# The first image's first eight score units taken from the unstacked parts, and its first value tiles moved behind four units

## What is computed

```python
xn = _group_norm(xf, gn_w, gn_b)
qkv = einsum('oc,bcl->bol', w_qkv, xn) + b_qkv[None, :, None]
q, k, v = ...                       # 8 heads of ch = 32 channels
weight = einsum('bct,bcs->bts', q * scale, k * scale)
weight = softmax(weight.astype(float32), axis=1)
a = einsum('bts,bcs->bct', weight, v)
h = einsum('oc,bcl->bol', w_proj, a) + b_proj[None, :, None]
x = xf + h
```

## Time and profile before

| | |
|---|---|
| median of 3 runs | 1343.61 us (1343.59 to 1346.18) |
| the profiled execution | 1351.87 us |
| its span, first to last instruction | 1350.1 us |
| TensorE busy | 1234.0 us (91%) |
| VectorE busy | 996.0 us (74%) |
| ScalarE busy | 878.0 us (65%) |
| mean granted TensorE clock | 0.984 of full |

### The profile page before, as it was taken

One profiled execution on the slowest core, in us unless ns is written; L12 is line 12 of the kernel. 1 busy time (PEld: TensorE's weight loads), 2 busy tenths in 40 slices (PEclk: granted clock), 3 DMA queues, 4 the chain that ended last, 5 costly groups with the idle time before them and its releaser, 6 DMA issues.

```text
span 1350.1 us, 22293 instructions
## 1 busy us (share of the span) xinstructions
PE 1234.0 (91%) x8028; PEld 646.0 (48%) x8028; DVE 996.0 (74%) x1609; ACT 878.0 (65%) x1457; POOL 466.6 (35%) x621
## 2 busy tenths in 40 slices
PE   6888899899998999899998999989998999979898
PEld 5544544544445454444444444454544444444465
DVE  3677688847888587866888578884879678794583
ACT  1567677676776668576775767766686767757332
POOL 2001017510384015630275203840156301751161
PEclk9999999999999999999999999999999999999999
DMA  8142325133442236223451234422362234410210
GB/s 275 47 123 67 98 59 114 25 68 117 100 108 59 46 99 141 49 63 94 98 114 25 66 118 100 108 50 49 106 141 49 63 94 99 81 27 0 80 33 32
DMA packets 51181, 110.86 MB, mean 82 GB/s; under 512 B 15456, under 2 KB 15840, under 8 KB 50816
## 3 DMA queue, kind: packets, MB, share of 16 engines
q1 hardware_dynamic: 48400, 100.39, 30.5%
q0 software_dynamic: 2480, 8.78, 2.3%
q10 hardware_dynamic: 192, 0.26, 0.1%
HBM read 21.81 MB, written 8.39 MB: 22 GB/s over the span
## 4 chain that ended last, share of the span: by engine, by line
PE 52%; DVE 29%; ACT 8%; issue 5%; POOL 3%; SPq 2%; DMA 1%; DVEq 0%; POOLq 0%; ACTq 0%
DVE negmax L1069 15%; PE ps_s L666 12%; PE ps_o L681 7%; PE work L754 6%; ACT probs L930 5%; PE work L693 5%; PE work L815 4%; PE work L740 4%; PE work L820 3%; PE work L705 3%; DVE tok L1145 3%; DVE ln_st L1134 3%; PE work L796 1%; DVE lo L1114 1%; PE work L728 1%
## 5 line engine op out<-in xcount | busy, mean ns | idle before, releaser
L1069 DVE TENSOR_REDUCE negmax<-ps_s 128x1 f32<-128x1024 f32 x512 | 619.4, 1214 | 219.2 <-PE ps_s L666 217.6
L930 ACT ACTIVATE probs<-ps_s,negmax 128x1024 f32<-128x1024 f32 x512 | 570.0, 1114 | 319.6 <-DVE negmax L1069 315.0
L666 PE MATMUL ps_s<-q_st,k_st 128*128 128x512 f32 x1024 | 407.3, 481 | 51.3 <-ACT probs L930 39.0
L666 PEld LDWEIGHTS ps_s<-q_st,k_st 128*128 128x128 f32 x1024 | 163.8, 191 | 294.0 <-ACT probs L930 161.2
L1347 POOL TENSOR_TENSOR v_scaled<-v_tok,rsums 128x128 f32<-128x128 f32 x128 | 55.9, 437 | 572.7 <-DVE rsums L1075 572.7
L681 PE MATMUL ps_o<-probs,v_scaled 128*32 128x512 f32 x2048 | 250.0, 606 | 1.3 <-POOL v_scaled L1347 1.3
L693 PE MATMUL work<-xg,w_qkv 128*128 128x512 f32 x256 | 121.0, 597 | 2.9 <-ACT xg L943 2.8
L754 PE MATMUL work<-ln_ch,w_qk 128*128 128x512 f32 x236 | 113.1, 601 | 3.4 <-DVE k_ch L1253 3.4
L681 PEld LDWEIGHTS ps_o<-probs,v_scaled 128*32 128x32 f32 x2048 | 53.8, 110 | 128.6 <-issue 116.6
L1406 POOL TENSOR_TENSOR x<-x,csum 128x1024 f32<-128x1024 f32 x45 | 107.5, 2389 | 2.5
L930 ACT ACTIVATION_READ_ACCUMULATOR probs<-ps_s,negmax 128x1 f32 x512 | 99.5, 194 | 0.0
(11 more groups left out here) (165 smaller groups left out, 1445.5 us busy)
## 6 DMA issues: line engine op xcount, KB each, us to landing
q_st<-hi SPq DMA_DIRECT2D x128, 128.0 KB, 2.4
q_st<-lo SPq DMA_DIRECT2D x120, 128.0 KB, 2.4
k_st<-t SPq DMA_DIRECT2D x224, 64.0 KB, 2.0
k_st<-hi SPq DMA_DIRECT2D x128, 64.0 KB, 2.0
k_st<-lo SPq DMA_DIRECT2D x128, 64.0 KB, 2.0
x<-in_x SPq DMA_DIRECT2D x8, 1024.0 KB, 6.0
out_x<-ln_ch SPq DMA_DIRECT2D x16, 512.0 KB, 2.8
xg<-in_x POOLq DMA_DIRECT2D x7, 1024.0 KB, 8.6
```

The lines of the kernel that those rows point to most:

```text
L666: mm = pe.matmul(ps_s[s % 2][:, half * HALF:half * HALF + HALF], k_st[:, h, j * P:j * P + P], q_st[g][:, h, half * HALF:half * HALF + HALF ...
L930: act.activation(probs[:, j % 2, h, :], ps_s[s % 2][:, :], ACT.Exp, bias=negmax[:, s % 4:s % 4 + 1], accum_out=sums[:, j % 2, h:h + 1]).th ...
L1069: dve.tensor_reduce(negmax[:, s % 4:s % 4 + 1], ps_s[s % 2][:, :], AX_X, ALU.max, negate=True)\
```

## The change

Four edits, all of the first image:

1. Units 0 to 7 (`DIRECT = 2 * HG`) are scored from `hi`, `lo`, `hi_first` and `lo_first` themselves: for each half of the queries four products of 32 rows by 512 columns accumulate in PSUM, so eight products stand for two. They wait for the parts in SBUF and not for the stacking DMAs. The stacked tensors are first read by unit 8. All DMAs stay.
2. The two tiles `pv0` leave the prologue of TensorE and VectorE. TensorE makes them in slots 3 and 4 of the first body, behind the scores of units 4 and 5; VectorE adds their bias behind the maxima of units 4 and 5.
3. `pv1` moves from TensorE's slot 0 (both parts) to slots 5 and 7, and on VectorE from slots 1 and 3 to 6 and 8. The warm entries of slots 0 to 4 go.
4. `hi_first` and `lo_first` lie in `q_st[1]` in place of `att`. So SyncE, before it stacks the second head group's queries of the first image, waits until the later half of the keys has been stacked.

```diff
-    "w1": (25, 27), "pq1": (11, 12), "pv1": (0, 0), "pk1": (19, 20), "gn": (39,), "pq0": (43, 44),
+    "w1": (25, 27), "pq1": (11, 12), "pv1": (5, 7), "pk1": (19, 20), "gn": (39,), "pq0": (43, 44),
...
-    "warm": (0, 1, 2, 3, 4, 5, 7, 8, 9, 13, 15, 16, 17, 21, 23, 24, 28, 29, 31, 32, 33, 35, 36, 37, 40, 41, 47, 48, 51, 52, 53, 57, 59, 60, 61),
+    "warm": (5, 7, 8, 9, 13, 15, 16, 17, 21, 23, 24, 28, 29, 31, 32, 33, 35, 36, 37, 40, 41, 47, 48, 51, 52, 53, 57, 59, 60, 61),
...
-    "invert": (4, 8, 12, 16, 20, 24, 28, 32, 36, 40, 44, 48, 52, 56, 60), "w1": (27, 29), "pv1": (1, 3),
+    "invert": (4, 8, 12, 16, 20, 24, 28, 32, 36, 40, 44, 48, 52, 56, 60), "w1": (27, 29), "pv1": (6, 8),
...
+DIRECT = 2 * HG
+VALUES_LATER = {HG - 1: ("pv0", 0), HG: ("pv0", 1)}
...
-        hi_first, lo_first = (att[:, n, :].bitcast(F32R) for n in range(2))
+        hi_first, lo_first = (q_st[1][:, n, :] for n in range(2))
...
         def stack_q(eng, b, g):
             eng.wait_ge(lo_done, 8 * b + 4 * g + 2)
+            if first_k(b, 0) and g == 1:
+                eng.wait_ge(k_stacked_b, 16 * DMA)
...
                 if first_k(i, g):
-                    if j == 0:
+                    if s < DIRECT:
+                        direct_scores(s, j, h)
+                        return
+                    if j == DIRECT // HG:
...
+            def direct_scores(s, j, h):
+                pe.wait_ge(lo_done, 1 + max(nth_split(0, t) for t in (("pk0", 0), ("pq0", 0), ("pq0", 1))))
+                if s >= 2:
+                    pe.wait_ge(probs_ready, s - 1)
+                rows, keys = slice(D * h, D * h + D), slice(P * j, P * j + P)
+                for half in range(2):
+                    cols = slice(half * HALF, half * HALF + HALF)
+                    for n, (k_part, q_part) in enumerate(((hi_first, hi), (lo_first, hi), (hi_first, lo), (lo_first, lo))):
+                        mm = pe.matmul(ps_s[s % 2][:, cols], k_part[rows, keys], q_part[rows, cols],
+                                       start=(n == 0), stop=(n == 3))
+                mm.then_inc(scores_ready, 1)
...
-                for tile in FIRST_TILES:
+                for tile in FIRST_TILES[:5]:
...
+                    if kind == "first" and s in VALUES_LATER:
+                        writing["body"] = -1
+                        pre_tile("prologue", -1, VALUES_LATER[s])
+                        writing["body"] = i
...
-                for tile in FIRST_TILES[1:]:
+                for tile in FIRST_TILES[1:5]:
...
+                    if kind == "first" and s - 1 in VALUES_LATER:
+                        writing["body"] = -1
+                        values(-1, VALUES_LATER[s - 1])
+                        writing["body"] = i
```

## The result

The changed kernel takes 1357.51 us (median of 6 runs, 1354.89 to 1362.92), the kernel before 1346.64 us beside it: ratio 1.0082, 95% interval 1.0063 to 1.0101. Its profiled execution took 1355.6 us with a span of 1353.8 us and a mean clock of 0.985.

A forecast was written before the change was run, and what follows sets the result against it. Query-stacking DMAs, then slow `pv1`, bound the first 50 us. The 6.85 us head start is spent by unit 9 (50.28 against 50.24); unit 11 gains 0.3 us: 1343.61 - 0.3 = 1343.3 us, range 1341.8 to 1347.8.

The forecast's parts named there:

- What bounded the stretch before: First 50 us: 7.94 us of DMA for stacked queries, then 5.22 us of `pv1` at the slow level, before unit 2.
- The price of a 32-row product: Direct units on TensorE: 0.23 us a product taken, between bounds of 0.213 and 0.31.
- Rivals 1: Direct units: slower by a dearer 32-row product; at 0.31 us each the time is 1346.5 us; chance 0.12.
- rival 3: Direct units: slower, weight loads not hidden within a row group, 40 x 0.11 = 4.4 us, 1347.7 us; chance 0.06.
- Rival 4: Direct units: faster, 32-row products run side by side and the 6.85 us head start is kept, 1336.8 us; chance 0.05.
- The changes of array form: Units 4 to 9 on TensorE: eight changes of form at about 0.1 us each, 0.8 us together.
- the gain of 0.3: Unit 11 at 53.56 us against 53.85 before, a gain that stays to the end of the kernel.
- The six warm pairs: Removed from slots in which TensorE waited: 2.6 us of TensorE work whose removal costs nothing.
- the slow stretch goes: 30 to 40 us: low clock should go, TensorE's pauses being only 25.4 to 26.9 and 30.5 to 31.6; sum at full clock.
- Rival 2: Direct stretch: slower by the clock; low throughout adds 8 us for products, 3.5 for value tiles (2.71 a pair), 1354.8; chance 0.05.
- SyncE's new wait and the stacking DMAs were covered: First image: wait ends about 44 us, parts behind it exist after 60; stacked queries issued at 31.19, needed at 47.5.
- nothing waits for a time of its own: Behind unit 11 the programs are the same, so the 0.3 us gain stays to the end.

The follow-up runs named there:

- e1: Changed kernel, but each product of a direct unit takes all 128 rows instead of its head's 32; 1.0018 of the kernel before.
- e3: Changed kernel with the direct scores alone, value tiles and warm entries back in their old places; 1.0096 of the kernel before.
- e6: The changed kernel, unchanged, run again for a second profile; 1.0069 of the kernel before.
- e9: Changed kernel with small 128-row filler products behind each of the first four direct units; 1.0079 of the kernel before.
- e7: Changed kernel with four direct units (0 to 3) in place of eight, all else the same; 0.9973 of the kernel before.
- e12: Changed kernel with four direct units and value tiles moved to TensorE's pauses, second run of that version; 0.9964 of the kernel before.

## Why the prediction was wrong

- What bounded the stretch before (DMAs, then `pv1` at the low clock), and that the waits go: right. Unit 0 began at 21.18 (forecast 21.57), unit 2 at 26.82 (26.95).
- The price of a 32-row product, 0.23 us: right at full clock, a unit being 1.84 us without its changes of form. Rivals 1 and 3, which stood on a dearer product, fall. All eight products of a unit are in one row group, and their loads are hidden at steps of 0.23. The trace so disagrees with the rule on weight loads that rival 3 came from (the Trainium skill, "TensorE: Matmul & The Clock Gate", Part 3, The mechanism). Rival 4 is half right: such products do run side by side, but those of two units and not of one, and off the path.
- The changes of array form: mis-sized. A direct unit is 2.03 and a value tile 1.98 in the chains, 4.01 a pair; in e1, where the form stays, a pair takes 3.63 (unit 5 at 34.70, unit 6 at 38.33). That is 0.19 for each change, not 0.1: 0.7 us over eight. With this alone the gain of 0.3 would have been a loss of 0.4, still no change. The six warm pairs that go are five, which cost nothing either way.
- **The step that failed** is the sentence that the slow stretch goes "since TensorE's pauses are now" short, with a sum made at full clock. It put the lower clock at nothing. Measured, it stretched a direct unit from 2.04 to 3.75 us and a value tile from 1.98 to 3.70, for 13.7 us in one profile and 30.7 in the other, and so put unit 11 5.1 and 13.3 us behind. I took pauses as the cause of a low clock. In e1 there are pauses and the clock is full; in e3 there is none and it falls and stays low. What differs in e1 is that the products use all 128 rows.
- Rival 2 had the mechanism's effect (low for the whole direct stretch, 1354.8 us) but not its cause, and so a chance of 0.05. It priced 11.5 us, and the medians say 10.9 and 6.3; the two profiles, at 5.1 and 13.3 us, lie around it. That is partly luck. Its value tile of 2.71 us is half of a term that ran only in part at the lower level; one wholly at that level takes 3.70. With five units at 1.71 and four tiles at 1.72 more, the whole stretch at the lower level would be 15.4 us, and no profile had all of it there.
- Behind unit 11 nothing gave the time back: right. SyncE's new wait and the stacking DMAs were covered: right, the distance to the kernel before is 5.1 us at unit 11 and still 5.1 at unit 63. That "nothing waits for a time of its own" behind it is too strong, as stays at the lower level come and go there.

The Trainium skill says on the clock ("TensorE: Matmul & The Clock Gate", Part 1, What's actually happening) that a monitor sets it by how busy the engine has been. Read as the busy share of the trace, that rule would give the direct units of e3 the full clock, and e3 disagrees: 5.00 of 5 us busy at 0.50.

What stays open: how often the low stretch is some 14 and how often some 30 us, as each kernel has one or two profiles; why the part behind unit 11 differs by up to 10.8 us between profiles, which is where the moved value tiles alone lost their 0.4%; what ends a low stretch, for the same units with value tiles between them ran at the lower level in e6 and at the full one in e9; and whether rows are the only thing that differs between the 32-row and the 128-row products, for e1 also stays in one array form and no products run side by side in it.

## What to carry to other kernels

Before a 128-row product is split into products of 32 rows to get round a wait, price the stretch at the lower clock too: a TensorE that is fully busy with narrow products can run at half speed for as long as they last, and drags the full-width work between them along. Use such products as a bridge only (here four units, not eight), and look at the granted clock of the stretch beside the busy share. Full-width work that is due anyway can go between them: with it unit 11 came at 48.5 and 45.3 and not at 52.1, though the timed ratios of e7 and e12 can't be told apart. Compare several executions of a stretch whose clock can fall; one profile of each showed a third of the loss.

## What the hardware showed that I had not expected

- TensorE busy without a gap for over 20 us at a granted clock of 0.50, three quarters of it in 32-row products (e3), after a fall that no pause went before, against 1.00 with 128-row products and pauses (e1).
- At the lower level TensorE's terms in the path take 1.8 to 1.9 times as long: a unit 3.75 against 2.04 us, a value tile of 16 records 3.70 against 1.98.
- Products of 32 rows of two heads run side by side without being asked to: in the changed kernel unit 1's first four run beside unit 0's last four.
- A change between the 32-row and the 128-row form costs about 0.19 us.
- The same program had a low stretch of 13.7 us in one execution and of 30.7 in another, with 8.2 us between them at unit 11.
